# A two-layer windowed feed-forward stage: two looped layers rewritten as one unrolled sequence of eight items in four overlapped parts

## What is computed

```python
def _layer(x, wqkv, qs, ksc, wo, lg, lb, w1, b1, w2, b2):
    h = shift_token(x)                    # features 64..127 come from the token before
    q, k, v = split(h @ wqkv, 3)          # 8 heads of 64
    q, k = l2norm(q) * qs, l2norm(k) * ksc
    q, k = rotary_xpos(q, k)
    o = local_attention(q, k, v)          # windows of 64, each sees itself and the one before
    x = x + o @ wo
    h = shift_token(x)
    h = (h - mu) / sqrt(var + 1e-05) * lg + lb
    a, g = split(h @ w1 + b1, 2)          # 341 each
    return x + (a * gelu(g)) @ w2 + b2
```

## Time and profile before

| | |
|---|---|
| median of 3 runs | 1715.23 us (1713.53 to 1715.48) |
| the profiled execution | 1712.0 us, of which the span is 1710.0 us |
| local feed-forward, first shift to last output | 243.0 to 586.7 us |
| its layer end, to the second half of the transpose | 586.8 to 593.6 us |
| mean granted TensorE clock over the span | 0.90 of 2.4 GHz |

### The profile page before, as it was taken

One profiled execution on the slowest core, in us unless ns is written; L12 is line 12 of the kernel. 1 busy time (PEld: TensorE's weight loads), 2 busy tenths in 40 slices (PEclk: granted clock), 3 DMA queues, 4 the chain that ended last, 5 costly groups with the idle time before them and its releaser, 6 DMA issues.

```text
span 1710.0 us, 24805 instructions
## 1 busy us (share of the span) xinstructions
PE 1382.2 (81%) x8770; PEld 865.1 (51%) x8815; DVE 1063.3 (62%) x2380; ACT 707.3 (41%) x2003; POOL 395.0 (23%) x308
## 2 busy tenths in 40 slices
PE   7999767777777656756688755889989899989997
PEld 4666535554455422222255434555556566656664
DVE  3556676664667568988876777765566455553333
ACT  4554324544444354555345411452224555432222
POOL 1333013222332033544640012400010233310000
PEclk9999988998899856666999887999999999999999
DMA  8000000000000220000000000000000000000000
GB/s 342 1 1 2 0 0 1 0 0 1 1 0 0 106 93 0 0 0 1 0 2 2 0 1 1 2 1 1 0 1 2 1 1 1 1 1 1 0 0 12
DMA packets 4205, 24.82 MB, mean 15 GB/s; under 512 B 1168, under 2 KB 3216, under 8 KB 3472
## 3 DMA queue, kind: packets, MB, share of 16 engines
q1 hardware_dynamic: 4112, 23.59, 3.4%
HBM read 23.06 MB, written 0.52 MB: 14 GB/s over the span
## 4 chain that ended last, share of the span: by engine, by line
PE 57%; DVE 18%; issue 16%; POOL 4%; ACT 4%; DMA 1%; DVEq 0%; POOLq 0%; SPq 0%; ACTq 0%
PE PS L1067 5%; PE PS L637 5%; PE PS L1052 4%; PE PS L1053 4%; PE PS L321 4%; PE PS L353 3%; PE PS L333 3%; PE PS L703 3%; DVE arena L2090 2%; PE PS L294 2%; PE PS L302 2%; PE PS L362 2%; POOL arena L2718 2%; PE PS L296 2%; PE PS L315 2%
## 5 line engine op out<-in xcount | busy, mean ns | idle before, releaser
L545 POOL TENSOR_TENSOR arena<-arena,small 128x768 f32<-128x768 f32 (+1 forms) x64 | 107.7, 1683 | 225.2 <-DVE small L488 116.0
L873 DVE TENSOR_REDUCE arena<-PS 128x2 f32<-128x512 f32 (+1 forms) x192 | 108.9, 609 | 53.2 <-PE PS L631 52.2
L800 ACT ACTIVATE arena<-PS 128x512 f32<-128x512 f32 (+1 forms) x192 | 92.2, 532 | 107.0 <-PE PS L637 107.0
L1156 DVE TENSOR_TENSOR arena<-arena,PS 128x512 f32<-128x512 f32 x82 | 56.4, 688 | 115.9 <-ACT arena L1089 115.9
L2146 POOL TENSOR_TENSOR arena<-arena 128x512 f32<-128x512 f32 x64 | 103.9, 1644 | 90.1 <-DVE arena L2081 36.0
L1089 ACT ACTIVATE arena<-PS 128x512 f32<-128x512 f32 x82 | 49.0, 597 | 165.8 <-PE PS L1053 165.8
L425 ACT ACTIVATE arena<-PS,small 128x256 f32<-128x256 f32 (+1 forms) x256 | 110.6, 452 | 0.0
L637 PE MATMUL PS<-arena 32*128 32x256 f32 (+1 forms) x768 | 97.5, 370 | 13.8 <-DVE arena L873 9.5
L2081 DVE TENSOR_TENSOR_SCAN arena<-arena 128x512 f32<-128x512 f32 x64 | 94.0, 1474 | 21.2 <-ACT arena L1979 13.8
L631 PE MATMUL PS<-arena 32*128 32x256 f32 (+1 forms) x768 | 94.5, 371 | 2.3 <-DVE arena L873 1.6
L1884 PE MATMUL PS<-arena,w_consts 128*128 128x512 f32 x128 | 91.2, 809 | 4.3 <-DVE arena L2090 4.3
(11 more groups left out here) (413 smaller groups left out, 3195.8 us busy)
## 6 DMA issues: line engine op xcount, KB each, us to landing
w_last<-in_last SPq DMA_DIRECT2D x1, 8260.0 KB, 23.6
w_rest<-in_rest SPq DMA_DIRECT2D x1, 5898.5 KB, 35.5
w_last<-in_first SPq DMA_DIRECT2D x1, 4532.5 KB, 20.8
w_last<-in_first SPq DMA_DIRECT2D x1, 2176.0 KB, 9.8
X<-in_x SPq DMA_DIRECT2D x1, 512.0 KB, 4.5
CT<-in_ctxT SPq DMA_DIRECT2D x1, 512.0 KB, 10.5
out<-X SPq DMA_DIRECT2D x1, 512.0 KB, 3.2
w_consts<-in_consts SPq DMA_DIRECT2D x1, 373.0 KB, 3.3
```

The lines of the kernel that those rows point to most:

```text
L545: g.tensor_tensor(p, p, ri, ALU.mult).then_inc(self.pn_done.sem, 1)
L873: v.tensor_reduce(dst, src, AX.X, ALU.max, negate=True).then_inc(self.mx_done.sem, 1)
```

## The change

The two objects become one, `LocalLayers`, with N = 8 items: items 0 to 3 are the batches of the first depth, 4 to 7 those of the second. `turns()` yields eleven turns m; in turn m each engine's list holds the first group of item p = m, attention steps 0 to 2 of item q = m-1 (and scores, maxima and exponentials of step 3), the last part of attention, output, residual and statistics of item r = m-2, and the feed-forward of item z = m-3. There are no loops on any engine.

Item 4 needs what item 0 has written; the shifted transpose of it (`XH`) is written by `back` in turn 3, and `project(4, 0)` waits for it (`xs_ev`) in turn 4. The other changes:

- The shifted tokens of all batches are kept in `XH`; at the start they are made by two large copies and a memset in place of two copies for each item. The rotary tables of both depths are built at the start (24 small VectorE instructions in place of 12 and 12).
- Queries are stored as they are (`QT`), without zero rows; a score product then has 64 rows and 64 columns of weights. VectorE copies the queries (2 copies an item, before 4), ScalarE the keys (2 copies, before on VectorE).
- `values` makes eight products of 64 by 64 in place of four of 128 by 128, straight into the place where one copy (`out`) takes them; before, two copies of 64 rows.
- `transposes` and `values` share one bank of PSUM (2), so `transposes` waits for the `out` of the step before.
- The sum with b2 moves from VectorE to GpSimd (`biased`), and for the second depth the x of the layernorm is added there too.
- Gate and up products of a part share a bank; `V` lies in the memory of weights that are no longer needed.
- `LayerEnd` is now `early` here: the last turn holds the statistics, root and normalization of tiles 0 to 5.

The core of the diff:

```diff
+    def turns(self):
+        for m in range(self.N + 3):
+            yield [n if 0 <= n < self.N else None for n in (m, m - 1, m - 2, m - 3)]
...
-                    ins = pe.matmul(PS[64 * r:64 * r + 64, k % 2, w * P:(w + 1) * P],
-                                    self.QZ[:, 2 * k + r, w * 64:w * 64 + 64],
-                                    self.KT[:, k, self.KEYS[w]:self.KEYS[w] + P],
-                                    start=False, stop=True, skip_group_check=True)
+                    rows = slice(64 * r, 64 * r + 64)
+                    ins = pe.matmul(PS[rows, k % 2, w * P:(w + 1) * P], self.QT[rows, k, w * 64:w * 64 + 64],
+                                    self.KT[rows, k, self.KEYS[w]:self.KEYS[w] + P], start=False, stop=True,
+                                    skip_group_check=True)
...
+            if g:
+                pe.wait_ge(self.o_ev.sem, self.o_ev.at(0, g))
             for w in range(4):
-                ins = pe.transpose(PS[:, 2 + k % 2, w * P:(w + 1) * P], self.Pr[:, k % 3, w * P:(w + 1) * P], c.ident)
+                ins = pe.transpose(PS[:, 2, w * P:(w + 1) * P], self.Pr[:, g % 3, w * P:(w + 1) * P], c.ident)
...
             for w in range(4):
-                ins = pe.matmul(PS[:, 4 + k % 2, w * P:(w + 1) * P], self.V[:, self.KEYS[w] // 64, k * P:(k + 1) * P],
-                                self.PT[:, k % 2, w * P:(w + 1) * P], start=True, stop=True)
+                for r in range(2):
+                    h = k * P + 64 * r
+                    ins = pe.matmul(PS[64 * r:64 * r + 64, 2, w * 64:w * 64 + 64],
+                                    self.V[:, n % 2 * 3 + self.KEYS[w] // 64, h:h + 64],
+                                    self.PT[:, g % 2, w * P + 64 * r:w * P + 64 * r + 64], start=True, stop=True,
+                                    skip_group_check=True)
...
+        def out(n, k):
+            a.wait_ge(self.o_done.sem, self.o_done.at(0, 4 * n + k + 1))
+            a.activation(self.OT[:, k, :], PS[:, 2, 0:256], ACT.Copy).then_inc(self.o_ev.sem, 1)
```

916 lines of the change are left out of this document (493 added, 423 removed).

## The result

The changed kernel takes 1649.5 us (median of 4 runs, 1648.1 to 1651.5), the kernel of before 1715.4 in the same session: a ratio of 0.9616 with a 95% interval of 0.9600 to 0.9633. The forecast was 1646. The profiled execution took 1648.05 us, of which the span is 1646.3.

What follows compares the result with a forecast made beforehand. The stage was taken as bound by a chain from engine to engine, no engine full. Turns summed to 277.2 us, 281.2 with the layer end against 350.6, saving 69.4: 1642.6 profiled, 3.2 more for the median, 1646 us (1634 to 1660).

Steps and rivals of the forecast that it cites:

- Values and scores taken at nothing: Edits inside attention: a values group stays 0.85 us by its weight loads, a scores group 1.09, so no gain.
- The walk: One chain through a full turn's engine lists, with 0.5 us added for short waits: 32.3 us, 31.5 in turn 7.
- C: Full turn: shift 0.8, gelu 0.5, table load 1.28, exponentials 1.5, ending at 14.8 us; VectorE stands over 2 at the reciprocal.
- D: Full turn: sums 0.65, rotate 1.3, hidden 0.5, down product 1.5, ending at 19.1 us.
- F: Full turn: refinement 0.9 and two multiplications of 1.11, ending at 26.75 us.
- G: Full turn's end: maxima, spread 1.3, step 3 exponentials 1.5, shifted transpose 0.8, key copies 0.6 each, transposes 0.65, ending 31.8.
- Of the early split nothing is left over: Layer end falls from 6.8 to about 4 us, but its early tiles add 1.9 and 0.7 to the last turn.
- 1: Row tiles writing one bank don't run together: scores 0.6 us more a group, 10 in all, 1656; chance 0.12.
- 2: Engine lists hold each other up more: 5 us a turn in the six fullest turns, 1676; chance 0.14.
- 3: Hops are shorter and small overlaps better: a turn at 29.5 us, 1626 in all; chance 0.08.
- 4: TensorE stays at its lower clock, 1.2 GHz, throughout: 47 us a turn, 1785 in all, slower than before; chance 0.02.
- 5: Items can't overlap because each waits for the one before, so no gain: 1712 to 1716 us; chance 0.02.

Runs made afterwards that it cites:

- the filled kernel: The changed kernel with 14 identity transposes added in each of turns 1 to 8, before TensorE's wait for the probabilities of step 1: 1644.2 us, ratio 0.9591.

## Why the prediction was right, step by step

- **The bound.** A chain through in-order lists, nothing full: right. The work of a turn of 31.5 us takes 43.8 with attention apart (where the attention is slower by itself, too), and 28.6 with two pieces of code in another order. TensorE, busy for 25.3 us of these 28.6, is near the bound only there.
- **Work of an item.** VectorE 22.4 forecast, 21.5 measured (under the 22 to 23 that the profile was to show); ScalarE 19 and 19.0; GpSimd under 13.3 and 12.9; TensorE 23.5 as a sum of records, 25.4 in the windows.
- **Values and scores taken at nothing.** Scores right: 1.09 us. The Trainium skill, "TensorEngine Tiling (Array Packing)", Restrictions and Gotchas, says that different row tiles can't be at one bank at the same time; 64-row products into one bank took as long as 128-row ones, so the trace contradicts the cost that I drew from it. Values mis-sized: I had 0.85 from the loads of the scores, 0.9 to 1.1 with the tail of the last; measured are 0.69 with the tail, with 16 loads in 0.55. The step that failed is "the loads then set the time: 0.85 as before": sixteen loads of 64 columns took 0.85 only where products of 128 columns stood between them, so it seems that they followed the products and didn't set the pace. The 0.053 us a load that I read there was then the products' pace; "nothing shrinks further than this" was wrong, at 0.034 a load here. With the saved copy the edit is worth 3 to 5 us where I had nothing, and over half of that in the profiled pair is one turn with a low clock.
- **The walk.** 32.3 forecast for turns 3 to 6; measured 31.5, 31.5, 33.2, 31.5, and 32.3 for turn 7 (31.5 forecast). Their sum with turns 1 and 2 is 211.8 against 211.7 forecast. The marks of the walk hold. In turn 4, from the first score product: the reciprocal of step 1 at 15.1 us (end of C: 14.8), the end of the down product at 19.1 (D: 19.1), the end of the multiplications at 26.6 (F: 26.75), the next scores at 31.5 (G: 31.8). Two things cancel in it: the terms of part G add up to 5.45 and not to the 5.05 that the sum has, and the 0.5 added for short waits wasn't there. That the sum of the turns is so close is luck in part: turns 3, 4 and 6 are 0.8 us under the forecast, and turns 5 and 7, by the clock, and 1 and 2, each a little longer than forecast, gave it back. The two holds that it named are real: (C), 2.31 us at the reciprocal (table loads away: -7.7; gates earlier: -6.7), and (G), the maxima and exponentials of step 3 (moved: -15.3).
- **The granted clock.** "Over 0.95 in full turns" failed in two of five, which show 0.95. The step that failed is the comparison of the length of TensorE's stands (2.2 us at most) with those of before, taken as safe: the clock fell behind stands of 1.8 us in turns 5 and 7, and in the filled kernel without one. The first two falls cost 1.7 us each (33.2 against 31.5, and 32.4 against 30.7 with the filler, from mask to mask). Turn 5, at 33.2, is also outside the 31 to 33 that the profile was to show.
- **Turn 0**, 19.5 forecast, 21.3 measured. Kernel after: the first rotation, and the projections behind the next.

```profile
247.91 0.68 DVE L2603 TENSOR_TENSOR arena<-PS,arena 128x512 f32<-128x512 f32 x1
...
249.93 2.48 PE L2260 MATMUL PS<-w_last,arena 128*128 128x512 f32 x3 [2.70 <-ACT arena L2462]
```

  The tables and the shift cost 1.4 us, not 2.2 (first rotation 3.8 us after the start, before 2.4), and the fewer copies gave 1.4 back (first transposes to first scores 5.1 in place of 6.5), the low end of the 1.4 to 2.8 forecast, of which the sum took 2.6. Not forecast: 1.4 us between them, where the projections ran at the lower clock (0.55 from 251 to 253 us).
- **Turn 8**, 22 forecast, 24.9 measured; the largest miss. I counted four steps of attention at 5.4 us one after the other and forgot that the feed-forward of item 5 and the last part of item 6 are in the same lists:

```profile
488.29 1.28 ACT L2548 ACT_TABLE_LOAD   x1
...
491.12 0.18 DVE L2638 RECIPROCAL small<-small 128x4 f32<-128x4 f32 x1 [3.31 <-ACT arena L2486]
...
492.47 0.66 PE L2310 MATMUL PS<-w_consts,arena 128*128 128x128 f32 x4 [2.75 <-POOL arena L2785]
...
493.18 2.43 PE L2378 MATMUL PS<-w_last,arena 128*128 128x128 f32 x12
```

  Hold (C) is here too, 3.31 us, and the 2.75 us stand of TensorE is followed by products at the lower clock (2.43 in place of 1.60). From the first scores to the transposes of step 3 the turn takes 24.6 us; in the kernel with attention apart the same stretch, with nothing beside it, takes 16.9. (What was expected for that kernel calls the 24.9 us of turn 8 "attention alone"; they aren't.)
- **Turns 9 and 10 and the layer end**: 12, 12 and 4 forecast, 12.8, 10.6 and 3.7 measured. "Of the early split nothing is left over" is neither shown nor refuted: the kernel without it takes 1.4 us more, within the noise.
- **The sum**: 281.2 forecast, 285.1 measured (+1.8 in turn 0, +0.1 in turns 1 to 7, +2.9 in turn 8, -0.9 behind it). The profiled execution misses by more, 1648.05 against 1642.6, since the stage also started 1.1 us later and what lies behind it took 0.7 more. The median again misses by less, 1649.5 against 1646, since it lies 1.5 us above the profiled execution and not 3.2. That last part is luck.
- **The rivals.** 1 fell (scores); 2 and 3, turns of 37 or of 29.5 us, didn't come: full turns at the full clock are 0.8 under the forecast, turn 8 is 2.9 over it; 4 named a thing that is real, a lower clock, but for stretches of a few us and not throughout; 5 fell: the stage is 65.5 us shorter, and taking attention out of the overlap cost 78 us.

What stays open: why the clock falls behind a stand of 1.8 us in turns 5 and 7 and not in turns 3, 4 and 6, and why it falls at the end of turn 5 in the filled kernel. No run here settles it. Each kernel's turns are read from one profiled execution, so in which turn a low stretch lies in the others isn't known.

## What to carry to other kernels

When items are overlapped, the engines' lists become the schedule: look in a full turn for the two or three long waits of an engine that isn't the bound, see what short piece ahead of it in another list is late, and move that piece; here two such moves were worth 22 us, a third of what the whole change had brought. A turn with nothing else in it (the first, the last) must be walked through the same lists as a full one, not summed up from its own chain. And where two turns with the same instructions differ, read the granted clock first: filling a stand of TensorE of under 2 us with products that nobody reads was worth 4 to 9 us here, in part because the clock stayed up and in part because its fall moved to where nobody waits for TensorE.

## What was not expected of the hardware

- The granted clock fell in turns whose longest stand of TensorE was 1.80 us, in 2 of 5 full turns of one kernel and in other ones of near variants; such a turn was 1.7 us longer. 14 transposes of the identity (1.75 us) in that stand brought the down product back from 2.70 to 1.60 us, but in that turn the clock then fell to 0.53 for 3.6 us at its end, behind stands of 0.82 us and less.
- Sixteen weight loads of 64 columns took 0.55 us between products of 64 columns, and 0.85 between products of 128.
- Eight score products of 64 rows by 64 columns, in pairs on different rows that write one bank, took 1.09 us, the same as with 128 rows each.
